# Two-layer hybrid attention block: running maxima read with a stride, a reciprocal taken two steps later, and a causal split placed ahead of a mask

## The reference, cut to what matters

```python
Q = (x @ Wq + bq).reshape(b, s, H, C) / 8          # K, V alike
scores = einsum('bshq,bshk->bshqk', Q, K)          # 64 x 64 numbers per head and token
scores = where(k > q, -inf, scores)                # causal inside the 64
w = softmax(scores, axis=-1)
attn = einsum('bshqk,bshk->bshq', w, V)
return attn.reshape(b, s, 1024) @ Wo + bo
```

## Time and profile before

| | us |
|---|---|
| median of three runs | 2248.83 |
| the profiled execution | 2247.19 |
| its span in the trace | 2245.5 |

### The profile page before, as it was taken

The page is one execution under the profiler, slowest core; times in us unless marked ns, Lnnn a source line. Parts: engine busy times, 40 slices in busy tenths (PEclk is TensorE's granted clock), DMA queues, the critical chain, the costliest instruction groups (busy, mean ns, idle before and its releaser), DMA issues. The chain is left out here.

```text
span 2245.5 us, 35597 instructions
## 1 busy us (share of the span) xinstructions
PE 1893.1 (84%) x14176; PEld 1405.2 (63%) x14226; DVE 1888.0 (84%) x1607; ACT 1106.6 (49%) x1448; POOL 1415.5 (63%) x661
## 2 busy tenths in 40 slices
PE   2899999999565978889889898888888989889886
PEld 1344444443253767767778787776777777777785
DVE  6877888777345989989899899998999989999884
ACT  2366666666412454454545544445544555444540
POOL 5122222222113987978879788797897987979871
PEclk8899999999866999999999999999999989999996
DMA  3300000000000000000000000000000000000000
GB/s 96 61 7 6 8 8 8 5 5 1 1 0 0 1 1 1 1 2 1 1 2 1 1 1 2 1 1 2 1 1 2 1 1 1 2 1 1 1 1 19
DMA packets 10981, 14.46 MB, mean 6 GB/s; under 512 B 4656, under 2 KB 7632, under 8 KB 10672
## 3 DMA queue, kind: packets, MB, share of 16 engines
q1 hardware_dynamic: 9264, 11.31, 2.1%
q10 hardware_dynamic: 1536, 0.63, 0.1%
HBM read 4.57 MB, written 1.05 MB: 3 GB/s over the span
## 5 line engine op out<-in xcount | busy, mean ns | idle before, releaser
L1059 POOL TENSOR_TENSOR b_p_ring<-b_p_ring,b_m 128x2048 f32<-128x2048 f32 (+7 forms) x384 | 1251.4, 3300 | 244.3 <-DVE b_p_ring L969 243.0
L1097 ACT ACTIVATE b_p_ring<-b_p_ring 128x2048 f32<-128x2048 f32 (+7 forms) x384 | 532.3, 1411 | 654.1 <-POOL b_p_ring L1059 652.5
L1160 PE MATMUL b_ps<-k_ident,b_ev_ring 128*128 128x128 f32 (+6 forms) x4608 | 606.5, 283 | 162.9 <-DVE b_ev_ring L1017 157.5
L1160 PEld LDWEIGHTS b_ps<-k_ident,b_ev_ring 128*128 128x128 f32 (+6 forms) x4608 | 510.0, 139 | 237.2 <-DVE b_ev_ring L1017 211.2
L1017 DVE TENSOR_TENSOR b_ev_ring<-b_p_ring,b_ps 128x2048 f32<-128x2048 f32 (+7 forms) x384 | 634.1, 1655 | 5.7 <-PE b_ps L1126 4.0
L969 DVE TENSOR_TENSOR b_p_ring<-b_ps,b_key 128x2048 f32<-128x2048 f32 (+7 forms) x384 | 634.4, 1660 | 0.0
L1160 PE MATMUL b_ps<-k_ident,b_p_ring 128*128 128x128 f32 (+6 forms) x4608 | 588.0, 279 | 18.3 <-ACT b_p_ring L1097 12.6
L1160 PEld LDWEIGHTS b_ps<-k_ident,b_p_ring 128*128 128x128 f32 (+6 forms) x4608 | 521.9, 138 | 28.5 <-ACT b_p_ring L1097 12.9
L547 ACT ACTIVATE a_ex<-a_ps 128x512 f32<-128x512 f32 (+3 forms) x768 | 333.0, 497 | 200.5 <-PE a_ps L492 191.0
L564 DVE TENSOR_REDUCE a_negm<-a_ps 128x1 f32<-128x768 f32 (+7 forms) x384 | 353.3, 953 | 75.6 <-PE a_ps L453 72.7
L384 POOL TENSOR_SCALAR_AFFINE_SELECT a_ex<-a_ex 128x512 f32<-128x512 f32 x128 | 81.6, 638 | 372.6 <-ACT a_ex L547 371.1
(11 more groups left out here) (163 smaller groups left out, 1076.8 us busy)
## 6 DMA issues: line engine op xcount, KB each, us to landing
rk_of_group<-rows_k SPq DMA_DIRECT2D x96, 32.0 KB, 2.0
rq<-rows_q SPq DMA_DIRECT2D x42, 64.0 KB, 2.4
k_wqkv<-in_wqkv SPq DMA_DIRECT2D x1, 2048.0 KB, 8.5
out<-x_all SPq DMA_DIRECT2D x4, 256.0 KB, 2.4
k_wo<-in_wo SPq DMA_DIRECT2D x1, 512.0 KB, 9.3
rq<-rows_q SPq DMA_DIRECT2D x12, 32.0 KB, 1.9
k_w_attn<-in_w_attn ACTq DMA_DIRECT2D x1, 192.0 KB, 2.8
k_reset_max<-in_reset_max ACTq DMA_DIRECT2D x1, 128.0 KB, 4.8
```

The costliest lines, as they stand in the source:

```text
L1059: nc.gpsimd.tensor_tensor(pc, pc, over_rows(m[:, half].rearrange("p i h -> p (i h)"), c), ALU.subtract).then_inc(shifted.sem, 1)
L1097: nc.scalar.activation(pc, pc, ACT.Exp).then_inc(exp_done.sem, 1)
L1160: last = nc.tensor.matmul(ps[0:width, bank, b // IB * P:(b // IB + 1) * P], rows[:, r, b:hi].rearrange("p i h -> p (i h)"), k["ident"][:], ...
```

## The change

- In `phase_b`, `turn_back`, its two tiles and its semaphore are gone. `maxima` reads `kmax` and `kmin` directly, head by head, in reversed query order: neighbouring elements of that read are 64 floats (256 bytes) apart.
- The scratch of `maxima` is now the bank of the summed `p` of the same half (bank 5 or 7) in place of bank 1, and the two waits that guarded bank 1 are gone. PE waits before the keys by head for ACT's copies of the keys.
- `finish` of half 1 goes from step 3 to step 5, `project` from 4 to 6, `residual` from 6 to 8. ACT's `invert` stays where it was (`INVERT1_AT` 4, `INVERT0_AT` 20).
- Keys go to steps 9 and 11, ACT's copies of them to 12 and 14, keys by head to 14 and 16, the scans to 15 and 17.
- In `phase_a2`, `EARLY` is 7 and `EARLY_ROWS` 5 (before 5 and 3), and POOL issues `split` ahead of the mask of `at` = 9.

```diff
--- before.py
+++ after.py
@@ -321,7 +321,7 @@
         U, G = len(units), len(groups)
         STEPS = 4 * G
         ST_SLOTS, ST_BANK, O_BANK, ITEM_BANK = 3, 0, 3, 4
-        EARLY, EARLY_ROWS, TURN_ITEM, PAD_ITEM = 5, 3, 6, 8
+        EARLY, EARLY_ROWS, TURN_ITEM, PAD_ITEM = 7, 5, 6, 8
         DIAGONAL = [at for at, (half, sbk) in enumerate(groups) if sbk * P >= 512 * half]
         masked = sem("masked", len(DIAGONAL))
         ready = sem("ready")
@@ -409,11 +409,11 @@
             split(0)
             for n in range(JOBS):
                 for at in DIAGONAL:
+                    if at == 9 and n + 1 < JOBS:
+                        split(n + 1)
                     mask(n, at)
                     if at == 2 and n >= 1:
                         combine(n - 1)
-                    if at == 9 and n + 1 < JOBS:
-                        split(n + 1)
             combine(JOBS - 1)
             pool.wait_ge(out_step.sem, out_step.at(JOBS - 1, 2))
 
@@ -874,9 +874,9 @@
     Q_BANK, T_BANK, V_BANK, ACC_BANK = 0, 1, 2, 4
     HALF = HID // 2
     INVERT0_AT, INVERT1_AT = 20, 4
-    FINISH0_AT, FINISH1_AT, PROJECT_AT, RESIDUAL_AT = 19, 3, 4, 6
-    XT_AT, KEY_AT, KEY_TAKEN_AT = 5, (7, 9), (10, 12)
-    HJ_AT, SCAN_AT, TURN_BACK_AT = (13, 15), (14, 16), 18
+    FINISH0_AT, FINISH1_AT, PROJECT_AT, RESIDUAL_AT = 19, 5, 6, 8
+    XT_AT, KEY_AT, KEY_TAKEN_AT = 5, (9, 11), (12, 14)
+    HJ_AT, SCAN_AT = (14, 16), (15, 17)
     Q1_AT, Q0_AT, V1_AT, V0_AT = 11, 19, 16, 23
     with ExitStack() as ctx:
         sb = lambda n, s, d=F32: ctx.enter_context(nc.sbuf_tensor("b_" + n, s, d))
@@ -887,8 +887,6 @@
         key = sb("key", [P, 2, C, H])
         kmax = sb("kmax", [P, HID])
         kmin = sb("kmin", [P, HID])
-        kmaxr = sb("kmaxr", [P, C, H])
-        kminr = sb("kminr", [P, C, H])
         m = sb("m", [P, 2, FIRST, H])
         rden = sb("rden", [P, 2, HALF])
         oT = sb("oT", [P, 2, HALF])
@@ -911,7 +909,6 @@
         key_taken = sem("key_taken", 2)
         hj_psum = sem("hj_psum", 2)
         scan_done = sem("scan_done", 4)
-        turned_back = sem("turned_back", 2)
         m_step = sem("m_step", 6)
         q_psum = sem("q_psum", 2)
         v_psum = sem("v_psum", 2)
@@ -978,17 +975,16 @@
                 nc.vector.tensor_tensor_scan(kmin[:, cols], k["reset_min"][:, 0:HALF], ps[:, T_BANK], 0.0,
                                              ALU.max, ALU.min).then_inc(scan_done.sem, 1)
 
-            def maxima(it, half, last=False):
+            def maxima(it, half):
 
                 q = ps[:, Q_BANK].rearrange("p (i h) -> p i h", h=H)
-                t = ps[:, T_BANK].rearrange("p (i h) -> p i h", h=H)
-                at = lambda r: r[:, half * FIRST:(half + 1) * FIRST, :]
+                t = ps[:, ACC_BANK + 2 * half + 1].rearrange("p (i h) -> p i h", h=H)
+                back = slice(C - 1, C - 1 - FIRST, -1) if half == 0 else slice(FIRST - 1, None, -1)
+                at = lambda r: r[:].rearrange("p (h c) -> p c h", h=H)[:, back, :]
                 dve.wait_ge(q_psum.sem, q_psum.at(it, half + 1))
-                dve.wait_ge(turned_back.sem, turned_back.at(it, 2))
-                if half == 1 and not last:
-                    dve.wait_ge(key_taken.sem, key_taken.at(it + 1, 2))
-                nc.vector.tensor_tensor(m[:, half], q, at(kmaxr), ALU.mult).then_inc(m_step.sem, 1)
-                nc.vector.tensor_tensor(t, q, at(kminr), ALU.mult).then_inc(m_step.sem, 1)
+                dve.wait_ge(scan_done.sem, scan_done.at(it, 4))
+                nc.vector.tensor_tensor(m[:, half], q, at(kmax), ALU.mult).then_inc(m_step.sem, 1)
+                nc.vector.tensor_tensor(t, q, at(kmin), ALU.mult).then_inc(m_step.sem, 1)
                 dve.wait_ge(m_step.sem, m_step.at(it, 3 * half + 2))
                 nc.vector.tensor_tensor(m[:, half], t, m[:, half], ALU.max).then_inc(m_step.sem, 1)
 
@@ -1017,7 +1013,7 @@
                     nc.vector.tensor_tensor(chunk(ev_ring, c), chunk(p_ring, c), over_queries(values(c), c),
                                             ALU.mult).then_inc(ev_done.sem, 1)
                     if begins:
-                        maxima(coming[0], BEGIN.index(coming[2]), last)
+                        maxima(coming[0], BEGIN.index(coming[2]))
                         multiply(*coming, first and c + AHEAD < N)
                     if not first and c == FINISH1_AT:
                         finish(it - 1, 1)
@@ -1076,12 +1072,6 @@
                 act.wait_ge(invert_step.sem, invert_step.at(it, 2 * half + 1))
                 nc.scalar.activation(rden[:, half], rden[:, half], ACT.Exp, scale=-1.0).then_inc(invert_step.sem, 1)
 
-            def turn_back(it):
-
-                act.wait_ge(scan_done.sem, scan_done.at(it, 4))
-                for straight, back in ((kmax, kmaxr), (kmin, kminr)):
-                    nc.scalar.copy(back[:], straight[:].rearrange("p (h c) -> p c h", h=H)[:, ::-1, :]).then_inc(turned_back.sem, 1)
-
             def take_xt(it, buf):
                 nc.scalar.copy(xt[:, buf], xnT[:, bass.ds(it * P, P)]).then_inc(xt_ready.sem, 1)
 
@@ -1099,8 +1089,6 @@
                         invert(it - 1, 1)
                     if c == INVERT0_AT:
                         invert(it, 0)
-                    if not last and c == TURN_BACK_AT:
-                        turn_back(it + 1)
                     if not last and c == XT_AT:
                         take_xt(it + 1, 1 - buf)
                     if not last and c in KEY_TAKEN_AT:
@@ -1113,7 +1101,6 @@
             take_xt(0, 0)
             for part in range(2):
                 take_key(0, 0, part)
-            turn_back(0)
             all_tiles(act, tile)
             invert(TILES - 1, 1)
 
@@ -1187,7 +1174,7 @@
                         queries(it, buf, 1)
                     if not last and c in HJ_AT:
                         if c == HJ_AT[0]:
-                            pe.wait_ge(m_step.sem, m_step.at(it, 6))
+                            pe.wait_ge(key_taken.sem, key_taken.at(it + 1, 2))
                         keys_by_head(it + 1, 1 - buf, HJ_AT.index(c))
                     if not last and c == V1_AT:
                         pe.wait_ge(ev_done.sem, ev_done.at(it, 16))
```

## The result

The changed kernel took 2156.1 us, median of four runs (2155.1 to 2157.7), against 2248.9 us of the kernel before: ratio 0.959 (95% interval 0.957 to 0.961), 4.1% faster. The forecast was 2159.5 us, range 2135 to 2188. The profiled execution took 2155.5 us with a span of 2153.8 us, 91.7 us less than before. The first layer norm of the feed-forward block that follows stage A begins at 606.1 us (before 613.3), and that of the block after stage B at 2098.3 us (before 2189.7). So **7.2 us came from stage A and 84.2 us from stage B**. One execution of a later experiment (turn_in_halves: 2703.4 us, granted clock 0.65) was in a slower state and stands in no ratio.

The account below looks back on a forecast made before the run. DVE was taken to bound stage B, PE stage A's inner loop. Span 2245.5 - 105.2 (waits) + 3 (queries) + 24.3 (stride) - 11.5 (stage A) = 2156.1; plus 1.7 and 1.6, 2159.5 us; range 2135 to 2188.

Parts of the forecast that it names:

- Half 1: Stage B, step 3: DVE's wait for ACT's reciprocal goes whole in fifteen tiles, 48.1 us less.
- POOL late next: Stage B: POOL's chain runs without slack, DVE's margin at value product 12 falls to 2.5 us, DVE does not wait.
- POOL paces half 0: Rival, stage B: the half-1 wait returns as waits for exponentials in steps 5 to 15; 48.1 us lost, 2208 us; 7%.
- Half 0: Stage B, step 19: without `turn_back` the reciprocal is there 1.7 us early; 15 waits of 3.55 us go, 53.2 us.
- the half-0 wait stays: Rival, stage B: POOL, trailing into half 1, eats the 1.7 us margin; 53.2 us lost, 2213 us; 5%.
- Queries late next: Stage B, before `maxima`: PE's query matmuls end with thin margin; 3 us allowed, bounds nothing and 21 us.
- The strided read: Stage B, `maxima`: 64 DVE instructions at ACT's strided time per element cost 0.38 us more each, 24.3 us.
- free: Rival, `maxima` in stage B: DVE hides the stride; 24.3 us less, 2135 us; 10%.
- by ratio: Rival, `maxima` in stage B: the read costs ACT's strided-to-contiguous ratio, 40 us in all, 2175 us; 12%.
- the slower one: Rival, `maxima` in stage B: the read is as slow as line 592 seems, 179 us, 2314 us; 3%.
- Bank and semaphores: Stage B: moved scratch bank and PE's new wait for ACT's key copy cost nothing, between 0 and 1 us a tile.
- Stage A: PE's waits for POOL's `split` go, 19.4 us; 4.5 given back for heavier items, 3.4 for start and job 14: 11.5 less.

Follow-up runs that it names:

- turn_in_halves: Changed kernel with ACT turning the scans' results back in four 512-element copies, behind the reciprocal of step 20 and in step 21: 2133.0 us, ratio 0.9502.
- finish1_at_3: Changed kernel with `finish` of half 1 back in step 3, `project` and `residual` left in 6 and 8: 2211.5 us, ratio 0.9851.
- turned_by_act: Changed kernel with ACT's two turning copies back, all in step 18, and `maxima` reading the turned tiles: 2211.1 us, ratio 0.9849.
- b_only: Kernel before with the stage-B edits alone: 2160.9 us, ratio 0.9619.
- a_split_only: Kernel before with only POOL's `split` moved ahead of the mask of `at` = 9, EARLY 5 and EARLY_ROWS 3: 2230.6 us, ratio 0.9931.
- turn_in_halves_split: turn_in_halves with EARLY 5, EARLY_ROWS 3, and `split` ahead of the mask of `at` = 9 except the last job's: 2117.2 us, ratio 0.9433.

## Why the prediction was right, and where its terms were off

- **Half 1 (48.1 us).** Right. finish1_at_3 brings 49.2 us of waiting back. The forecast arrival, 3.4 us after the reciprocal, is 3.3 us in the trace.
- **POOL late next.** Right that it has no break any more, and that DVE still doesn't wait: 2.5 us of margin at value product 12 were forecast and are there. The rival "POOL paces half 0" is out; finish1_at_3 excludes it by itself, since there a wait of DVE in step 3 shows in full; and in the changed kernel DVE waits 1.7 us in all for exponentials, as before.
- **Half 0 (53.2 us).** Right: the margin of 1.7 us read from the last tile, the only one without `turn_back`, is 1.67 us in an ordinary tile now. turned_by_act shows the cause. The rival "the half-0 wait stays" is out. Of the two waits that were to stay, that of half 0 in the last tile grew from 0.52 to 1.31 us.
- **Queries late next (3 us allowed).** The margins were as thin as feared, 0.27 and 0.13 us, but only one wait of 0.8 us came of them. 2.2 us over-allowed.
- **The strided read (24.3 us).** 64 instructions cost 34.0 + 33.7 us against 64 x 0.687: 23.7 us. Forecast per instruction 1064 ns, measured 1064 and 1053. The rivals "free" (684) and "by ratio" (1.31 us) are both out, as is the slower one. What carried over from ACT to DVE is the time per element, and not the ratio. The Trainium skill ("Vector Engine (DVE) Microarchitecture Reference", Measured stream behaviour on trn2) gives 1.73 ns where one source hops 4 KiB every element; its 1.75 ns, which the prediction put with it, is for both sources stepping by 72 or 152 words. By DVE's fixed 151 ns the trace has (1064 - 151) / 512 = 1.78 ns, which agrees within 3%. No run here steps by 24 words, so the 2.50 ns were not tried.
- **Bank and semaphores (nothing).** No run has this part alone. DVE's waits for the keys' matmul are 15.2 us before and after, both at the start of stage B, so no new wait came of it.
- **Not in the sum.** Waits of the value products for the values' matmul fell from 4.0 to 1.4 us. With the 3.9 us at the start, 100.6 + 3.9 + 2.6 - 23.7 - 0.8 = 82.6 of the 84.2 us that stage B gained; 77.9 were forecast.
- **Stage A (11.5 us forecast, 7.2 measured): the term that was mis-sized.** Of the 1.22 us wait of each job I gave back 0.3 us for the heavier items near the rows. Measured: the split's move is worth 1.38 us, a little more than the wait, and EARLY costs 0.85 us. The net 0.53 us over 13 equal jobs is 6.9 us. The start and job 14 were forecast to cost 3.4 us together; the first interval got 3.3 us shorter (29.03 for 32.34 us) and the last 3.0 us longer (35.88 for 32.90). So the equal jobs gave 8.0 us less than the forecast's 19.4 - 4.5, and the start and job 14 cost next to nothing together where 3.4 us were allowed: two misses that partly cancel. The first interval is not all the edit's: b_only, whose stage A is that of the kernel before, has 30.91 us there. The stall behind the split in job 14 came as described, 3.9 us of waiting on PE. I took it for granted that EARLY was needed for the earlier split to work. It was not: in a_split_only the split waits 0.36 us for the last maximum, the mask behind it begins 2.53 us after the one before it (2.46 in the kernel before), and PE waits for neither.

The error of stage A (4.3 us too much) and those of stage B (6.3 us too little) have opposite signs, so that the total is closer than its parts is luck: 2.3 us off in the span. The median is 3.4 us off, since the 1.6 us added for the step from the profiled execution to the median were 0.6.

**A bound that was none.** The upper bound of the strided read, 179 us, and the rival "slower" took line 592 as a slow strided read. Line 592 is a RECIPROCAL, and the kernel before has another one, of 256 elements that lie side by side:

```profile
599.17 1.75 DVE L652 RECIPROCAL a_ms<-a_ms 128x256 f32<-128x256 f32 x1 [0.48 <-ACT a_ms L668]
```

With the same 151 ns taken off, that is 6.2 ns per element, against 6.5 on line 592. The operation is what is slow there, not the stride, and the row could have taken this rival out before the result.

## What to carry to other kernels

When a wait on another engine is the gap of the bound engine, look at what stands in that engine's queue ahead of the awaited instruction, and for a stretch of the trace that happens to lack it: the last tile priced the removal to 0.1 us. Work taken off a side engine and put on the bound one is paid in full (25 us here) when the side engine only had it in the wrong place; moving it behind the urgent instruction gave both gains. And when two edits go together, time each alone: here one of them was worth 15.5 us, and the other cost 7 by itself and 9 on top of it.

## What the runs showed of the hardware

A VectorE instruction with one float32 source 256 bytes apart from element to element, the other source in PSUM and contiguous, ran at 1.78 ns per element (1.76 where the result goes to PSUM, line 987), and ScalarE's copy with the same pattern at 1.783 ns, though their contiguous rates differ (1.041 and 0.848 ns). The forecast had only taken this as the nearer of two readings; that the two engines agree within about 1% suggests that the read and not the engine is the limit, though nothing here shows what sets it. Halving that ScalarE copy to 512 elements gave 1098 and 1111 ns in turn_in_halves_split, for 1094 worked out from the fixed part and the slope.
